# Graph attention with exponentials left unscaled and inverse sums applied to the node products

## The chip, the cores and the metric

The kernel runs on 1 core of one Trainium2 chip, as one launch. The metric is the device time of the launch in microseconds (us); lower is better. The engines: PE (TensorE, with PEld its weight loads), DVE (VectorE), ACT (ScalarE), POOL (GpSimd), SP (SyncE, which here issues most DMAs). Each runs its own instructions in program order and waits for the others by semaphores.

## The reference, cut to what matters

Two graph transformer blocks over 625 nodes of width 768 and 20000 edges. The change lies in the graph attention of the second block, in the first of its two layers (8 heads of 128 columns):

```python
def gat_layer(x, W, att_src, att_dst, bias, src, dst, heads, out_ch, concat):
    n = x.shape[0]
    h = (x @ W.T).reshape(n, heads, out_ch)
    a_src = jnp.einsum('nhc,hc->nh', h, att_src)
    a_dst = jnp.einsum('nhc,hc->nh', h, att_dst)
    e = jax.nn.leaky_relu(a_src[src] + a_dst[dst], 0.2)
    m = jax.ops.segment_max(e, dst, num_segments=n)
    ex = jnp.exp(e - m[dst])
    denom = jax.ops.segment_sum(ex, dst, num_segments=n)
    alpha = ex / (denom[dst] + 1e-16)
    out = jax.ops.segment_sum(alpha[:, :, None] * h[src], dst, num_segments=n)
    ...
h = gat_layer(x, W1, ..., heads=8, out_ch=128, concat=True)
h = jax.nn.relu(h)
out = gat_layer(h, W2, ..., heads=1, out_ch=768, concat=True)
```

Before it the block has another attention (called mix here), and behind it a routed feed-forward layer of 8 experts, which takes about the second half of the time.

## The kernel before

**How the numbers are held.** Every 32-bit product on PE is made of three matmuls: each operand is a pair of a rounded upper half (made by ACT, `upper`, L358) and the rest (made by DVE, `lower`, L361: source minus upper half). `mm3` (L340) multiplies hi x hi, hi x lo, lo x hi. PE writes its results into 8 PSUM banks, handed out in turn by `ring.next`, which makes PE wait until the bank's last content was evicted.

**The graph attention as a dense one.** Nodes are padded to 640, 5 tiles (`TT`) of 128. Edge counts were made into a dense matrix of logs, `edge_log` (a tile of destinations by 640 sources). The first layer goes over 4 groups (`grp`) of 2 heads. In a group, a *unit* is one head and one tile of destinations: 10 units a group, 40 (`N1`) in all. Units of the same head are closed in *pairs* of `n` tiles (tiles 0 and 1, 2 and 3, and tile 4 alone), 6 a group, 24 in all.

**Steps of a unit**, with their lag in ticks behind the tick at which the unit enters (a tick is one turn of the loops over `i`, L2072, L2200 and L2372, which each engine has for itself):

- 0, ACT: raw edge scores by a Relu (`raw_edges`, L2170); POOL has added the source row to the edge logs (`terms`, L1999), a step that waits for the peak of two units before.
- 1, DVE: `peak` (L2329): joins the two, and finds minus the maximum.
- 2, ACT: `exponent` (L2176), with the row's sum into `total`.
- 3, DVE: sum + 1e-16, its reciprocal, times `has_edge` (L2396 to L2398).
- 4, ACT: the exponentials times that inverse, per destination, which lies on the partitions (L2232).
- 5, PE: five transposes (`turn_unit`, L2046), so that sources lie on the partitions.
- 6, ACT and DVE: upper and lower half of the transposed exponentials into `exT`, a spare part of the tiles `weight_hi` and `weight_lo` (so a row `weight_hi<-bank 128x384` is such a step, and `weight_hi<-weight_raw` is a weight's).
- 7, PE, at the last unit of a pair: the z product (L2093), nodes `hg` times `exT`, 15 matmuls; the result has the head's columns on the partitions and destinations along the free side.
- 8, ACT: Relu with bias (L2214) and upper half of z; DVE: lower half (`zT_lo`).

**Work put between, by tables of ticks:** the output projection of z by the second layer's weights (`Y_AT`, PE 12 matmuls a tile, DVE adds it), the node projections of the next group (`PREPARE`, PE 18 matmuls a step, ACT its upper half at L2158, DVE its lower half at L2301 and four dots for the scores), the turning and spreading of the source rows (`TURNED`, L2015; `SPREAD`, L354, L2145), and the splitting of weights into halves (`SPLIT`, L304, L314). Within a tick PE's order is: output projection, z product, source rows, transposes, node projections. ACT's is: z, upper halves of the exponentials, scaling, exponent, source rows, raw edges, projections, weights. DVE's is: lower half of z, lower halves of the exponentials, inverse sum, peak, output projection, node projection, weights. After the last tick the second layer begins with the scores of the last output projection.

## Time and profile before

| what | us |
|---|---|
| median of 3 runs | 1976.0 |
| lowest, highest run | 1969.53, 1976.93 |
| span of the profiled execution, first to last instruction | 1967.6 |
| PE busy in it | 1855.2 (94%) |
| DVE busy | 1295.7 (66%) |
| ACT busy | 934.8 (48%) |
| POOL busy | 151.5 (8%) |
| mean granted clock of PE | 0.973 of full speed |

How to read it: the shares are means over the whole program. The stage of the change takes about a tenth of it, and there the three engines are near each other; the stretches of that stage tell more than the table. Granted clock is the share of its full speed that the chip let PE run at; its two levels are 1.2 and 2.4 GHz. Ends of matmuls are modelled: durations of neighbours overlap, so the distance between two starts is the better price.

### The profile page before, as it was taken

The page shows a single profiled execution, that of the slowest core. Times are in us where ns is not written, and L with a number is a line of the kernel's source. Part 1 is how long each engine was busy: PE and PEld are TensorE (multiplying, and loading weights), DVE is VectorE, ACT ScalarE, POOL GpSimd, SP SyncE. Part 2 cuts the span into 40 slices and gives each one's busy share as a digit, 9 for nine tenths or more (in the row PEclk, how much of TensorE's full clock was granted, in tenths as well). Part 3 has the DMA queues.
Part 4 walks back from the last instruction along what each step waited for, and adds up shares of the span by engine and source line. Part 5 has one row for each costly group of instructions (what it writes and reads, how often), then busy time and mean ns, then how long its engine had stood idle before and what let it go on. Part 6 is the DMA issues. An engine that isn't in the chain of part 4 may idle for free.

```text
span 1967.6 us, 30950 instructions
## 1 busy us (share of the span) xinstructions
PE 1855.2 (94%) x12197; PEld 1758.9 (89%) x12198; DVE 1295.7 (66%) x2485; ACT 934.8 (48%) x1551; POOL 151.5 (8%) x127
## 2 busy tenths in 40 slices
PE   6987999999999999788799999999999999999998
PEld 5876789998889999787699999999999999999998
DVE  7997767555345656888865744456566667676886
ACT  2331222325134536878534232345555556666776
POOL 0000000004000023323100000000101001001010
PEclk9997999999999999899799999999999999999999
DMA  3110002101112112010131132154656566676795
GB/s 117 49 49 1 25 25 105 33 25 60 62 49 89 73 39 94 23 38 17 65 123 61 63 104 73 73 207 183 220 193 221 214 217 240 219 261 245 283 328 199
DMA packets 36844, 234.30 MB, mean 119 GB/s; under 512 B 5964, under 2 KB 7366, under 8 KB 14680
## 3 DMA queue, kind: packets, MB, share of 16 engines
q1 hardware_dynamic: 31366, 217.41, 30.8%
q0 software_dynamic: 2656, 8.99, 2.0%
q10 hardware_dynamic: 2674, 5.87, 0.8%
q8 instruction: 99, 1.62, 0.3%
q14 instruction: 49, 0.40, 0.1%
HBM read 221.91 MB, written 10.35 MB: 118 GB/s over the span
## 4 chain that ended last, share of the span: by engine, by line
PE 43%; issue 3%; DVE 3%; DMA 1%; ACT 1%; POOL 0%; ACTq 0%; POOLq 0%; DVEq 0%
PE bank L2734 8%; PE bank L341 7%; PE bank L342 7%; PE bank L343 7%; PE bank L2735 4%; PE bank L2746 3%; PE bank L2750 2%; PE bank L2738 2%; PE bank L2747 2%; PE bank L2749 1%; PE bank L2737 1%; DVE weight_lo L314 1%; PE bank L2692 0%; DMA out<-ffn_y,slot_token 0%; DMA weight_raw_fifth<-in_ffn_w 0%
## 5 line engine op out<-in xcount | busy, mean ns | idle before, releaser
L314 DVE TENSOR_TENSOR weight_lo<-weight_raw,weight_hi 128x2304 fp32r<-128x2304 f32 (+1 forms) x155 | 392.3, 2534 | 53.5 <-ACT weight_hi L304 53.2
L304 ACT ACTIVATE weight_hi<-weight_raw 128x2304 fp32r<-128x2304 f32 (+1 forms) x155 | 323.3, 2087 | 69.1 <-DMA weight_raw<-in_ffn_w 48.3
L341 PE MATMUL bank<-xT_hi,weight_hi 128*128 128x320 f32 (+1 forms) x576 | 182.8, 317 | 1.6 <-DVE xT_lo L362 1.4
L342 PE MATMUL bank<-xT_lo,weight_hi 128*128 128x320 f32 (+1 forms) x576 | 178.0, 309 | 0.0
L343 PE MATMUL bank<-xT_hi,weight_lo 128*128 128x320 f32 (+1 forms) x576 | 177.7, 309 | 0.0
L341 PE MATMUL bank<-weight_hi,xT_hi 128*128 128x384 f32 (+1 forms) x480 | 161.4, 336 | 11.2 <-DVE weight_lo L314 6.2
L3114 DVE TENSOR_TENSOR hidden_tmp<-hidden_tmp,bank 128x160 f32<-128x160 f32 (+5 forms) x192 | 65.6, 342 | 159.5 <-ACT hidden_tmp L2897 159.5
L342 PE MATMUL bank<-weight_lo,xT_hi 128*128 128x384 f32 (+1 forms) x480 | 157.3, 328 | 0.0
L343 PE MATMUL bank<-weight_hi,xT_lo 128*128 128x384 f32 (+1 forms) x480 | 157.0, 327 | 0.0
L615 PE MATMUL bank<-one_hot_dst,one_hot_src 125*128 125x313 f16 x800 | 123.5, 306 | 15.2 <-ACT packed_counts L629 7.9
L2897 ACT ACTIVATE hidden_tmp<-bank,ffn_b_by_load 128x160 f32<-128x160 f32 (+5 forms) x192 | 73.6, 404 | 119.8 <-PE bank L2738 114.2
L341 PE MATMUL bank<-weight_hi,hidden_hi 128*128 128x384 f32 (+1 forms) x366 | 124.7, 341 | 0.0
L342 PE MATMUL bank<-weight_lo,hidden_hi 128*128 128x384 f32 (+1 forms) x366 | 123.8, 338 | 0.0
L615 PEld LDWEIGHTS bank<-one_hot_dst,one_hot_src 125*128 125x128 f16 x800 | 75.0, 100 | 52.3 <-DVE one_hot_dst L587 17.3
L2734 PE MATMUL bank<-xT_hi,weight_hi 128*128 128x512 f32 (+3 forms) x390 | 117.3, 361 | 3.4 <-DVE hidden_tmp L3114 1.7
L343 PE MATMUL bank<-weight_hi,hidden_lo 128*128 128x384 f32 (+1 forms) x348 | 117.7, 338 | 0.0
L341 PEld LDWEIGHTS bank<-xT_hi,weight_hi 128*128 128x128 f32 x576 | 110.1, 191 | 7.1 <-issue 4.2
L2734 PE MATMUL bank<-xT_lo,weight_hi 128*128 128x320 f32 (+3 forms) x390 | 110.5, 350 | 5.9 <-DVE xT_hi L3069 4.9
L342 PEld LDWEIGHTS bank<-xT_lo,weight_hi 128*128 128x128 f32 x576 | 110.3, 191 | 0.0
L343 PEld LDWEIGHTS bank<-xT_hi,weight_lo 128*128 128x128 f32 x576 | 110.1, 191 | 0.0
L341 PEld LDWEIGHTS bank<-weight_hi,xT_hi 128*128 128x128 f32 x480 | 93.3, 194 | 13.4 <-DVE weight_lo L314 7.0
L2735 PE MATMUL bank<-xT_hi,weight_lo 128*128 128x256 f32 (+3 forms) x390 | 97.7, 250 | 0.0
(496 smaller groups left out, 5062.4 us busy)
## 6 DMA issues: line engine op xcount, KB each, us to landing
weight_raw<-in_ffn_w SPq DMA_DIRECT2D x111, 1152.0 KB, 5.1
weight_raw_fifth<-in_ffn_w SPq DMA_DIRECT2D x25, 1152.0 KB, 5.1
weight_raw<-in_shared_w SPq DMA_DIRECT2D x16, 1152.0 KB, 5.0
weight_raw<-in_mix_kv SPq DMA_DIRECT2D x8, 1152.0 KB, 5.0
weight_raw<-in_gat_w SPq DMA_DIRECT2D x8, 768.0 KB, 4.2
weight_raw<-in_mix_q SPq DMA_DIRECT2D x4, 1152.0 KB, 5.0
weight_raw<-in_mix_out SPq DMA_DIRECT2D x4, 1152.0 KB
weight_raw<-in_gnn_w SPq DMA_DIRECT2D x4, 1152.0 KB, 5.1
```

Of the source, the lines that this page charges most:

```text
L304: act.activation(upper_, whole_, ACT.Copy).then_inc(*w_hi.one())
L314: dve.tensor_tensor(lower_, whole_, upper_.bitcast(F32), ALU.subtract).then_inc(*w_lo.one())
L341: pe.matmul(dst, a[0], b[0], start=first, stop=False)
L342: pe.matmul(dst, a[0], b[1], start=False, stop=False)
L343: return pe.matmul(dst, a[1], b[0], start=False, stop=last)
L615: end = pe.matmul(edge_banks[t][:, 0:TM], hot_src[:, j % HOT, tok(t)], hot_dst[:, j % HOT, 0:TM], start=(i == 0), stop=(i == CHUNK_E - 1))
L2734: pe.matmul(both, hi[:, k, :], x_e[:, k, :, 0:width], start=(k == 0), stop=False)
L2735: pe.matmul(first, lo[:, k, :], x_e[:, k, 0, 0:width], start=False, stop=False)
L2738: end = pe.matmul(both, hi[:, k, :], x_e[:, k, :, 0:width], start=False, stop=True)
L2746: pe.matmul(both, hi[:, k, :], h[:, k, :, 0:width], start=(first and k == 0), stop=False)
L2897: act.activation(ht[:, i % 3, 0:CAPS[e]], r_banks[i][:, 0:CAPS[e]], ACT.Identity, bias=b1r[:, e, i % (3 * NCH):i % (3 * NCH) + 1]).then_in ...
L3114: dve.tensor_tensor(part, part, r_banks[i][:, width:2 * width], ALU.add).then_inc(*r_sum.one())
```

## The change

What it does:

- The exponentials are not scaled. The copy at lag 4 on ACT goes, and the transposes move from lag 5 to 3, the halves from 6 to 4, the z product from 7 to 5.
- Instead z is multiplied by the inverse sums. There the destinations lie along the free side, so the inverses are needed as rows, the same on all partitions: at lag 3, once a pair, DVE adds `least_sum` and takes the reciprocals of the pair's `n` sums; at lag 4 PE transposes each column, broadcast to 128 columns; at lag 5 ACT copies the bank into one tile, `inverse` (named `edge_terms` in rows, since it is a spare part of that tile); at lag 6 DVE multiplies z's bank with it into `zt`, ACT makes the Relu in place and the upper half, DVE the lower half.
- `least_sum`, made once, is 1e-16 where a destination has edges and 5e37 where it has none; it takes the place of `has_edge` in this layer. `has_edge` stays for the second layer.
- Node projections: ticks 5, 6, 7, 7, 8 of the first group and 4, 5, 5, 6, 7 of the two others, before 6, 6, 7, 7, 8 of each. Output projections stand 2 or 3 ticks earlier for the last three tiles of group 2 and all of group 3 (groups are counted from 0), and three weights are split 2 or 4 ticks later. The last lag is 8 instead of 10. The raw edges have 5 slots instead of 7, z's halves 3 instead of 2.
- On ACT, z's steps move behind the upper halves of the exponentials; on DVE the product stands first and z's lower half behind peak and sums.

```diff
@@ layout
+        least_sum = sb("gat_least_sum", [P, TT], F32, gat)
-        ZS, XS = 7, DEPTH
+        ZS, XS = 5, DEPTH
-        zT = pair("gat_zT", [P, 2, 2, 2 * P], gat)
+        zT = pair("gat_zT", [P, 3, 2, 2 * P], gat)
+        inverse = count_f32[:, 2 * TP:2 * TP + 2 * P]
@@ tables
-        LAST_LAG = 10
+        LAST_LAG = 8
-        PREPARE = {6: (0, 1), 7: (2, 3), 8: (4,)}
-        Y_AT = {10 * grp + tick: (grp, t) for grp in range(4) for t, tick in enumerate((12, 13, 18, 19, 21) if grp < 3 else (12, 13, 16, 17, 18))}
+        PREPARE = {5: (0,), 6: (1,), 7: (2, 3), 8: (4,)}, {4: (0,), 5: (1, 2), 6: (3,), 7: (4,)}
+        Y_AT = {10 * grp + tick: (grp, t) for grp in range(4) for t, tick in enumerate({2: (12, 13, 16, 17, 18), 3: (10, 11, 14, 15, 16)}.get(grp, (12, 13, 18, 19, 21)))}
-        SPLIT = {10: c0 + 2, 12: c0 + 3, 14: c0 + 4, 20: c0 + 5, 24: c0 + 6, 28: c0 + 7}
+        SPLIT = {10: c0 + 2, 12: c0 + 3, 18: c0 + 4, 20: c0 + 5, 28: c0 + 6, 30: c0 + 7}
@@ def tensor():
-                q = pair_closing(i, 7)
+                q = pair_closing(i, 5)
...
-                    bank = ring.next(z_relu.at(q + 1))
+                    bank = ring.next(z_scaled.at(q + 1))
...
-                u = unit(i, 5)
+                u = unit(i, 3)
                 if u is not None:
-                    turn_unit(u, e_scaled.at(u + 1))
+                    turn_unit(u, e_exp.at(u + 1))
+                q = pair_closing(i, 4)
+                if q is not None:
+                    grp, h, t0, n = pairs_of[q]
+                    pe.wait_ge(*e_summed.at(q + 1))
+                    bank = ring.next(inverse_kept.at(q + 1))
+                    inverse_banks.append(bank)
+                    for t in range(n):
+                        end = pe.transpose(bank[:, t * P:(t + 1) * P], total[:, grp % 2, h, t0 + t:t0 + t + 1].broadcast_to([P, P]), ident[:, :])
+                    end.then_inc(*inverse_full.one())
@@ def scalar():
-                q = pair_closing(i, 8)
-                if q is not None:
...
-                    act.activation(zt[:, q % 2, 0:n * P], z_banks[q][:, 0:n * P], ACT.Relu, bias=b1[:, 2 * grp + h:2 * grp + h + 1]).then_inc(*z_relu.one())
...
-                u = unit(i, 6)
+                u = unit(i, 4)
...
-                u = unit(i, 4)
-                if u is not None:
-                    grp, h, t = units[u][0:3]
-                    e = edge_w[:, u % ZS, :]
-                    act.wait_ge(*e_summed.at(u + 1))
-                    act.activation(e, e, ACT.Copy, scale=total[:, grp % 2, h, t:t + 1]).then_inc(*e_scaled.one())
+                q = pair_closing(i, 5)
+                if q is not None:
+                    n = pairs_of[q][3]
+                    act.wait_ge(*inverse_full.at(q + 1))
+                    if q:
+                        act.wait_ge(*z_scaled.at(q))
+                    act.activation(inverse[:, 0:n * P], inverse_banks[q][:, 0:n * P], ACT.Copy).then_inc(*inverse_kept.one())
+                q = pair_closing(i, 6)
+                if q is not None:
+                    grp, h, t0, n = pairs_of[q]
+                    act.wait_ge(*z_scaled.at(q + 1))
+                    z = zt[:, q % 2, 0:n * P]
+                    act.activation(z, z, ACT.Relu, bias=b1[:, 2 * grp + h:2 * grp + h + 1]).then_inc(*z_relu.one())
+                    act.wait_ge(*z_relu.now())
+                    if grp:
+                        act.wait_ge(*sums_before(q))
+                    upper(at(zT, ALL, z_slot(q), h, slice(0, n * P)), z).then_inc(*z_hi.one())
@@ def vector():
-                q = pair_closing(i, 8)
+                q = pair_closing(i, 6)
+                if q is not None:
+                    grp, h, t0, n = pairs_of[q]
+                    dve.wait_ge(*z_full.at(q + 1))
+                    dve.wait_ge(*inverse_kept.at(q + 1))
+                    if q >= 2:
+                        dve.wait_ge(*z_lo.at(q - 1))
+                    dve.tensor_tensor(zt[:, q % 2, 0:n * P], z_banks[q][:, 0:n * P], inverse[:, 0:n * P], ALU.mult).then_inc(*z_scaled.one())
+                u = unit(i, 4)
+                if u is not None:
+                    turned_lower(u, at(exT, ALL, u % XS, ALL, ALL))
+                u = unit(i, 1)
+                if u is not None:
+                    peak(u, *units[u][0:3])
+                if pair_closing(i, 3) is not None:
+                    grp, h, t0, n = pairs_of[pair_closing(i, 3)]
+                    sums = total[:, grp % 2, h, t0:t0 + n]
+                    dve.wait_ge(*e_exp.at(i - 3 + 1))
+                    own_step(dve.tensor_tensor(sums, sums, least_sum[:, t0:t0 + n], ALU.add))
+                    dve.reciprocal(sums, sums).then_inc(*e_summed.one())
                 if q is not None:
                     grp, h, t0, n = pairs_of[q]
                     dve.wait_ge(*z_hi.at(q + 1))
                     lower(at(zT, ALL, z_slot(q), h, slice(0, n * P)), zt[:, q % 2, 0:n * P]).then_inc(*z_lo.one())
-                u = unit(i, 3)
-                if u is not None:
-                    grp, h, t = units[u][0:3]
-                    tot = total[:, grp % 2, h, t:t + 1]
-                    dve.wait_ge(*e_exp.at(u + 1))
-                    own_step(dve.tensor_scalar(tot, tot, 1e-16, None, ALU.add))
-                    own_step(dve.reciprocal(tot, tot))
-                    dve.tensor_tensor(tot, tot, has_edge[:, t:t + 1], ALU.mult).then_inc(*e_summed.one())
```

How instructions stand in a row shows it better at two places. On ACT, tick 16 and the start of 17, before: z's Relu and upper half, two rounded pieces of turned exponentials, scaling (L2232), exponent, raw edges, and the projections of the next group but one:

```order
L2214 ACTIVATE gat_z<-bank,gat_b 128x128
L359 ACTIVATE gat_zT_hi<-gat_z 128x128
L359 ACTIVATE weight_hi<-bank 128x384
L359 ACTIVATE weight_hi<-bank 128x256
L2232 ACTIVATE gat_edge<-gat_edge,gat_total 128x640
L2176 ACTIVATE gat_edge,gat_total<-gat_edge,gat_minus_peak 128x640
L2170 ACTIVATE gat_edge<-gat_src_row,gat_dst_bias 128x640
L2158 ACTIVATE gat_h_hi<-bank 128x256 x2
L2214 ACTIVATE gat_z<-bank,gat_b 128x128
L359 ACTIVATE gat_zT_hi<-gat_z 128x128
```

On ACT in the change, tick 14 behind its halves and the start of 15 (L2234 copies the inverses, L2240 is z's Relu, L2188 the exponent):

```order
L2234 ACTIVATE edge_terms<-bank 128x128
L2240 ACTIVATE gat_z<-gat_z,gat_b 128x128
L359 ACTIVATE gat_zT_hi<-gat_z 128x128
L2188 ACTIVATE gat_edge,gat_total<-gat_edge,gat_minus_peak 128x640
L2180 ACTIVATE gat_edge<-gat_src_row,gat_dst_bias 128x640
L2168 ACTIVATE gat_h_hi<-bank 128x256
L359 ACTIVATE weight_hi<-bank 128x384
L359 ACTIVATE weight_hi<-bank 128x256
L2240 ACTIVATE gat_z<-gat_z,gat_b 128x128
L359 ACTIVATE gat_zT_hi<-gat_z 128x128
```

The copy of 640 columns is gone, a copy of 128 columns of inverses stands ahead of z, and one projection follows the raw edges where two did.

On DVE, tick 15 and the start of 16, before, with z's lower half ahead of the exponentials' lower halves, and three small steps ahead of each peak (ISA, L2329):

```order
L362 TENSOR_TENSOR gat_zT_lo<-gat_z,gat_zT_hi 128x256
L362 TENSOR_TENSOR weight_lo<-bank,weight_hi 128x384
L362 TENSOR_TENSOR weight_lo<-bank,weight_hi 128x256
L2396 TENSOR_SCALAR gat_total<-gat_total 128x1
L2397 RECIPROCAL gat_total<-gat_total 128x1
L2398 TENSOR_TENSOR gat_total<-gat_total,gat_has_edge 128x1
L2329 ISA gat_edge,gat_minus_peak<-gat_edge,edge_terms 128x640
L2329 ISA gat_minus_peak 128x1
L362 TENSOR_TENSOR gat_zT_lo<-gat_z,gat_zT_hi 128x128
```

And tick 14 in the change (L2404 is the product with the inverses, L2343 the peak, L2415 and L2416 the sums):

```order
L2404 TENSOR_TENSOR gat_z<-bank,edge_terms 128x128
L362 TENSOR_TENSOR weight_lo<-bank,weight_hi 128x384
L362 TENSOR_TENSOR weight_lo<-bank,weight_hi 128x256
L2343 ISA gat_edge,gat_minus_peak<-gat_edge,edge_terms 128x640
L2343 ISA gat_minus_peak 128x1
L2415 TENSOR_TENSOR gat_total<-gat_total,gat_least_sum 128x2
L2416 RECIPROCAL gat_total<-gat_total 128x2
L362 TENSOR_TENSOR gat_zT_lo<-gat_z,gat_zT_hi 128x128
L2313 TENSOR_TENSOR gat_h_lo<-bank,gat_h_hi 128x256
```

z's lower half moved from ahead of the peak to behind it and the sums, right ahead of the node projection's steps.

## Rows read from the trace of the kernel before

**Rows 1.** The page: the span of the profiled execution

```profile
span 1967.6 us, 30950 instructions
```

**Rows 2.** Stages: microseconds busy per engine (instructions), granted clock, DMA share, GB/s

```profile
773.19:797.08 23.89, 19.52 (x152) 18.60 (x150) 19.78 (x87) 19.27 (x42) 6.26 (x4) 0.93 0.65 227
797.08:848.91 51.83, 42.69 (x293) 40.59 (x292) 40.45 (x133) 40.43 (x86) 15.66 (x10) 0.90 0.00 1
848.91:901.13 52.22, 45.48 (x303) 42.70 (x304) 43.08 (x138) 42.44 (x89) 15.58 (x10) 0.91 0.12 42
901.13:965.60 64.47, 56.70 (x369) 53.40 (x368) 55.06 (x158) 48.67 (x106) 15.65 (x10) 0.94 0.09 27
```

**Rows 3.** Waits of PE, 773 to 966 us: waiter, releaser: total us, times, longest

```profile
PE bank L341 <- DVE weight_lo L362: 13.3, 10, 3.2
PE bank L2015 <- DVE gat_scores L2278: 2.9, 1, 2.9
...
PE bank L2046 <- ACT gat_edge L2232: 2.5, 2, 1.5
```

**Rows 4.** PE in order of time: start us, us, line, operation, shape [idle before]

```profile
860.46 0.71 PE L2046 MATMUL bank<-identity,gat_edge 128*128 128x128 f32 x5
860.92 0.42 PE L341 MATMUL bank<-weight_hi,gat_zT_hi 128*128 128x384 f32 x1
...
863.13 0.71 PE L2046 MATMUL bank<-identity,gat_edge 128*128 128x128 f32 x5
...
867.22 0.33 PE L341 MATMUL bank<-weight_hi,gat_h_hi 128*128 128x128 f32 x1 [0.37 <-DVE weight_lo L362]
...
868.95 0.74 PE L2046 MATMUL bank<-identity,gat_edge 128*128 128x128 f32 x5
872.91 0.33 PE L341 MATMUL bank<-weight_hi,gat_h_hi 128*128 128x128 f32 x1 [3.23 <-DVE weight_lo L362]
```

**Rows 5.** ACT in order of time, one tick and its z steps

```profile
869.47 0.75 ACT L359 ACTIVATE weight_hi<-bank 128x384 fp32r<-128x384 f32 x2
870.10 0.83 ACT L2232 ACTIVATE gat_edge<-gat_edge,gat_total 128x640 f32<-128x640 f32 x1
870.82 0.82 ACT L2176 ACTIVATE gat_edge<-gat_edge,gat_minus_peak 128x640 f32<-128x640 f32 x1
...
872.35 0.36 ACT L2214 ACTIVATE gat_z<-bank,gat_b 128x128 f32<-128x128 f32 x1
...
872.96 0.75 ACT L359 ACTIVATE weight_hi<-bank 128x384 fp32r<-128x384 f32 x2
```

**Rows 6.** DVE in order of time, columns as in rows 4

```profile
912.72 1.15 DVE L362 TENSOR_TENSOR gat_zT_lo<-gat_z,gat_zT_hi 128x256 fp32r<-128x256 f32 x1
...
917.57 0.14 DVE L2396 TENSOR_SCALAR gat_total<-gat_total 128x1 f32<-128x1 f32 x1
...
918.06 0.83 DVE L2329 CUSTOM_DVE_ANT_0 gat_edge<-gat_edge,edge_terms 128x640 f32<-128x640 f32 x1
...
918.82 0.42 DVE L362 TENSOR_TENSOR gat_zT_lo<-gat_z,gat_zT_hi 128x256 fp32r<-128x256 f32 x1
919.15 0.88 DVE L362 TENSOR_TENSOR weight_lo<-bank,weight_hi 128x384 fp32r<-128x384 f32 x2
```

**Rows 7.** POOL in order of time, beside them

```profile
912.02 1.57 POOL L1999 TENSOR_TENSOR edge_terms<-gat_edge_log,gat_src_row 128x640 f32<-128x640 f32 x1 [1.40 <-DVE gat_minus_peak L2329]
...
919.04 1.61 POOL L1999 TENSOR_TENSOR edge_terms<-gat_edge_log,gat_src_row 128x640 f32<-128x640 f32 x1 [1.41 <-DVE gat_minus_peak L2329]
```

**Rows 8.** The two stretches behind the 3.2 us waits, columns as in rows 2

```profile
821.90:826.00 4.10, 4.10 (x24) 4.10 (x25) 3.48 (x12) 4.07 (x9) 1.82 (x2) 0.64 0.00 0
872.90:877.00 4.10, 4.08 (x25) 4.09 (x26) 3.53 (x13) 3.05 (x7) 1.84 (x2) 0.66 0.00 0
```

**Rows 9.** Groups by shape: busy us, mean ns | idle before

```profile
L2301 DVE TENSOR_TENSOR gat_h_lo<-bank,gat_h_hi 128x256 fp32r<-128x256 f32 x15 | 6.3, 423 | 9.9 <-ACT gat_h_hi L2158 9.8
L2158 ACT ACTIVATE gat_h_hi<-bank 128x256 fp32r<-128x256 f32 x15 | 5.7, 383 | 19.7 <-PE bank L343 19.7
```

More of the change, by code:

```diff
@@ L1838, in graph_attention @@
          att_in, h_full, h_hi, h_lo, scored, score_turned, score_hi, score_lo, rows_full, rows_kept,
-         e_acted, e_made, e_exp, e_summed, e_scaled, ex_turned, ex_hi, ex_lo, z_full, z_relu, z_hi, z_lo,
+         e_acted, e_made, e_exp, e_summed, z_scaled, inverse_full, inverse_kept, ex_turned, ex_hi, ex_lo, z_full, z_relu, z_hi, z_lo,
          y_full, y_added, scored2, h2_hi, h2_lo, o_full, o_added) = sigs(*names)
@@ L1892, in graph_attention @@
         h_banks, turn_banks, row_banks, ex_banks, z_banks, y_banks, o_banks = [], [], [], [], [], [], []
+        inverse_banks = []
         units, pairs_of = [], []
@@ L1933, in preparations @@
             if i < N1 and i // 10 < 3:
-                for step in PREPARE.get(i % 10, ()):
+                for step in PREPARE[i >= 10].get(i % 10, ()):
                     yield i // 10 + 1, step
@@ L1944, in z_slot, with sums_before @@
         def z_slot(q):
+            return pairs_of[q][2] // 2
+        def sums_before(q):
             grp, h, t0, n = pairs_of[q]
-            return (3 * grp + t0 // 2) % 2
-        def sums_after(q):
-            grp, h, t0, n = pairs_of[q]
-            return y_full.at(2 * (grp * TT + t0 + n))
+            return y_full.at(2 * ((grp - 1) * TT + t0 + n))
         def w1_chunk(grp):
@@ L2175, in exponent @@
                 act.wait_ge(*e_made.at(u + 1))
+                if grp > 1 and t == 0:
+                    act.wait_ge(*aggregated(grp - 2))
                 act.activation(e, e, ACT.Exp, bias=minus_peak[:, grp % 2, h, t:t + 1], scale=-1.0,
@@ L2207, in scalar @@
                     act.dma_start(slots_dram[:, 0:D].rearrange("(t p) d -> p t d", p=P), x[:, :, :]).then_inc(*x_kept.dma())
-                q = pair_closing(i, 8)
-                if q is not None:
-                    grp, h, t0, n = pairs_of[q]
-                    act.wait_ge(*z_full.at(q + 1))
-                    if q >= 2:
-                        act.wait_ge(*z_lo.at(q - 1))
-                    act.activation(zt[:, q % 2, 0:n * P], z_banks[q][:, 0:n * P], ACT.Relu, bias=b1[:, 2 * grp + h:2 * grp + h + 1]).then_inc(*z_relu.one())
-                    act.wait_ge(*z_relu.now())
-                    if q >= 4:
-                        act.wait_ge(*sums_after(q - 4))
-                    upper(at(zT, ALL, z_slot(q), h, slice(0, n * P)), zt[:, q % 2, 0:n * P]).then_inc(*z_hi.one())
                 if i in Y_AT and Y_AT[i][1] == TT - 1:
@@ L2320, in edge_logs @@
                 dve.wait_ge(*dve_own.now())
+                own_step(dve.tensor_scalar(least_sum[:, :], edge_peak[:, :], -1.0, 5.0e37, ALU.is_lt, ALU.mult))
+                own_step(dve.tensor_scalar(least_sum[:, :], least_sum[:, :], 1e-16, None, ALU.add))
                 dve.tensor_scalar(has_edge[:, :], edge_peak[:, :], -1.0, None, ALU.is_ge).then_inc(*edges_known.one())
@@ L2387, in vector @@
                     lower(at(zT, ALL, z_slot(q), h, slice(0, n * P)), zt[:, q % 2, 0:n * P]).then_inc(*z_lo.one())
-                u = unit(i, 6)
-                if u is not None:
-                    turned_lower(u, at(exT, ALL, u % XS, ALL, ALL))
-                u = unit(i, 3)
-                if u is not None:
-                    grp, h, t = units[u][0:3]
-                    tot = total[:, grp % 2, h, t:t + 1]
-                    dve.wait_ge(*e_exp.at(u + 1))
-                    own_step(dve.tensor_scalar(tot, tot, 1e-16, None, ALU.add))
-                    own_step(dve.reciprocal(tot, tot))
-                    dve.tensor_tensor(tot, tot, has_edge[:, t:t + 1], ALU.mult).then_inc(*e_summed.one())
-                u = unit(i, 1)
-                if u is not None:
-                    peak(u, *units[u][0:3])
                 if i == FIRST_PART + 1:
```

4 lines of the change are left out of this document (2 added, 2 removed).

## The prediction

> **What bounds the kernel now.** Read first how long the stage takes and who is busy in it. One execution spans 1967.6 us [rows 1], and the loop that is changed lies between 773 and 966 us. In the three stretches from one spreading of source rows to the next, and on to the last output projection (51.83, 52.22 and 64.47 us), PE is busy 42.69, 45.48 and 56.70 us: it leads, but sits idle 9.1, 6.7 and 7.8 us, 23.7 us together. DVE follows with 40.45, 43.08 and 55.06, ACT with 40.43, 42.44 and 48.67 [rows 2]. So no engine is the bound throughout; it changes from tick to tick.
>
> Then read what PE waits for. The largest entry is the lower half of the turned exponentials, 13.3 us in 10 waits, the longest 3.2; the scores of the last node projection cost 2.9 once, and the scaled exponentials 2.5 in two [rows 3]. One of the 3.2 us waits is seen in order of time: PE ends its five transposes after 868.95 and begins the next z product only at 872.91 [rows 4]. DVE, named as releaser, is not the slow one: it subtracts what ACT has rounded, and ACT in these ticks runs without a gap. One tick of ACT goes from 869.47 to 872.35, 2.88 us: 0.63 for rounding the turned exponentials, 0.72 for the copy that scales them, and 1.53 for the exponent and the raw edges; the z steps of one tile add 0.61 [rows 5]. That is 3.5 us, while PE needs 1.73 for such a z product and about 0.46 for five transposes [rows 4]. In these ticks ACT is the bound; in the projection ticks PE is, since before two projections stood in one tick there.
>
> A gap costs a second time. Behind both 3.2 us waits the granted clock is 0.64 and 0.66 over 4.10 us [rows 8], the lower level (1.2 GHz) for most of it. Over the three stretches it is 0.90, 0.91 and 0.94 [rows 2].
>
> **The change, part by part.** The sum is made on the profiled execution; the median of the runs, 1976.0, lies 8.4 us above its span. A difference of less than 0.5%, 9.9 us, can't be told from none here. I put the difference on the median.
>
> 1. *The scaling copy goes.* 40 copies at 0.72 leave ACT, 28.8 us [rows 5]. In come 24 copies of spread inverses, nearest to the 256-column copy from a bank, 383 ns [rows 9], at most 9.2 us. An ACT tick falls from 2.88 to 2.16, with z steps and an inverse to about 3.2 at most. Then PE (z product, transposes, an output projection of 2.21 in some [rows 4]) or DVE is the longer. Both 3.2 us waits go: -6.4. Of the other 6.9 us of that entry (bounds 0 and 6.9) I take two thirds, since most are ACT ticks too and some are DVE's own: -4.6.
> 2. *Transposes take the exponentials unscaled*, two ticks earlier. The 2.5 us of waits on scaled exponentials can't stand as they do; the exponent is ready a tick before. -2.5, bounds 0 and -2.5.
> 3. *Clock.* With the two gaps go their slow stretches: 4.10 x 0.36 + 4.10 x 0.34 = -2.9 [rows 8]. Bounds: 0 if some other gap takes their place, and -13.8 if the clock never fell (0.10 x 51.83 + 0.09 x 52.22 + 0.06 x 64.47 [rows 2]).
> 4. *PE gains work.* 40 transposes of a broadcast column. Five transposes take 0.46 from 860.46 to 860.92 [rows 4], 0.09 each: +3.7. No cover: PE leads. The order has them behind the exponentials' transposes of the tick, so what is queued behind them are node projections and the next output projection.
> 5. *DVE.* Three small steps a unit go, 0.49 from 917.57 to 918.06 [rows 6], 40 times: -19.6. In come 24 products of a bank with the inverses, nearest to the 256-column subtraction from a bank, 423 ns [rows 9], and 24 pairs of small steps, two thirds of 0.49: 24 x (0.42 + 0.33) = +18.0. Even, before the next point. The two steps that make the least sums come ahead of the loop, while DVE waits for PE: nothing.
> 6. *DVE against POOL.* The subtraction that makes the lower half of z reads two tiles in SBUF. It took 0.42 where it began 0.22 ahead of POOL's sum, and 1.15 where it began 0.70 behind [rows 6, 7]: it waited till POOL was through. POOL starts just after each peak (its sum waits for it). Before, z's subtraction stood first in a tick, away from that. Now it stands behind peak and small sums. Right behind the peak it still comes first; where the sums lie between (two of six in a group, eight in all) it starts some 0.33 later, 0.1 behind POOL, and waits about 1.57 - 0.1 - 0.3 = 1.1 [rows 6, 7]. 8 x 1.1 = 8.8 on DVE; a quarter reaches PE, which leads: +2.2, bounds 0 and 24 x 1.1 = 26.4.
> The Trainium skill ("SBUF — State Buffer", section Who interferes with whom) says that a DVE instruction with two SBUF inputs and a GpSimd instruction that reads SBUF block each other wholly, and that the order of issue decides who. By that rule, the trace agrees, the product with the inverses, one input from a bank, is free of it, and the lower half of z is not.
> 7. *Node projections spread over ticks* (one, two, one, one instead of two, two, one), output projections moved to the ticks that lost a projection. Nothing is added; PE's own work stays, and it fills ticks in which PE waited. That gain is in term 1. The scores behind a projection take DVE the same time, and the 2.9 us wait before the first turned scores [rows 3] stays: there the last projection stands right ahead of it in both orders. Attention rows and weights land ahead of the earlier projections by several us: nothing.
> 8. *Lag 8 instead of 10.* No work less; two units' transposes and a z product come out of the tail into the first group, where PE works without them too. Nothing by itself.
>
> Sum: -6.4 - 4.6 - 2.5 - 2.9 + 3.7 + 2.2 = **-10.5 us**, 1976.0 - 10.5 = 1965.5.
>
> **Rivals.**
> *DVE becomes the bound.* If all six z subtractions of a group meet POOL (z's upper half is late, ACT now makes it behind a DVE step), DVE's busy time in the second stretch is 43.08 - 4.9 + 4.5 + 6 x 1.1 = 49.3, in the first 46.7 [rows 2, 6, 9]. With the 3 us that it can't fill anyway, since it waits for PE and ACT, that is 52.3 and 49.7 against 52.22 and 51.83: some 2 us gained, and 1 in the tail, which DVE nearly fills now (55.06 of 64.47). 1973. For it: DVE is busy only 2.2 and 2.4 us less than PE now. Against: a z's upper half has the time of rounding and peak, some 1.5 us, to get ready.
> *The waits go further and the clock stays up.* The idle 23.7 us fall by two thirds (15.8), 1.5 more ahead, and half of the 13.8 us of clock (6.9), less 3.7: -20.5, 1955.5. For it: loads of a tick are now near each other. Against: the gap at the first group's start, where the output weights are rounded at the same tick as before, stays and pulls the clock down there.
> *The longer z chain, slower.* z passed from PE to ACT; now PE's spread inverses are copied by ACT (0.38), DVE multiplies (0.42), and only then ACT has its z steps (0.61). There is one inverse tile and ACT takes its steps in order: while it waits for the product, exponent and raw edges are queued behind it, and PE waits for the exponent one tick on. Each of 24 pairs whose wait is exposed costs 0.38 + 0.42 + 0.61 = 1.41 [rows 5, 9]. It decides from 8 exposed pairs on (8 x 1.41 = 11.3 against 10.5). With 16: 22.6 - 10.5 = +12, 1988. Against it: DVE has the product first in its tick, and ACT rounds exponentials for 0.63 ahead of the wait.
>
> **How the numbers follow.** Forecast 0.5, with its own range 1959 to 1972; DVE bound 0.2 (1973); clock up 0.2 (1955.5); longer chain 0.1 (1988). The forecast lies just past the 0.5% line (1966.1), so its half is split, 0.28 faster and 0.22 same. Faster 0.28 + 0.2 = 0.48, same 0.22 + 0.2 = 0.42, slower 0.10. The range 1954 to 1977 leaves out the slower rival and a little below.
>
> **What would show it.** Right: no wait of 3 us in the middle of a group, a granted clock above 0.93 in the two middle stretches, each 3 us or more shorter than 51.83 and 52.22; ACT's busy share there down by 5 us a stretch; two of six z subtractions near 1.5 us and the others at 0.42. DVE bound: most of the six above 1 us and PE waiting for DVE's lower half as before. Longer chain: ACT idle ahead of z's Relu, released by DVE's product. Wrong altogether: stretches as long as before with ACT idle, or a new wait of PE for inverse sums.

## The result, and the profile after

| | before | after |
|---|---|---|
| median of 15 runs, us | 1970.56 | 1977.9 |
| lowest, highest | 1968.73, 1977.19 | 1972.53, 1982.03 |
| span of the profiled execution | 1967.6 | 1980.2 |
| ratio after to before, 95% interval | | 1.0033 [1.0024, 1.0043] |

The change makes the kernel 0.33% slower by the ratio, which is 6.5 us (the two medians lie 7.3 us apart), where 10.5 us less was forecast. The 1977.9 us lie outside the range of 1954 to 1977, though only by 0.9 us. That it is so near is luck: the forecast started from 1976.0, the median of 3 runs of the kernel before, and over 15 runs that median is 1970.56. As a change, the forecast missed by 17 us.

The page of the kernel after, its span (for rows 1) and the busy time of each engine:

```profile
span 1980.2 us, 31018 instructions
...
PE 1858.9 (94%) x12237; PEld 1763.4 (89%) x12238; DVE 1293.0 (65%) x2439; ACT 914.4 (46%) x1535; POOL 151.5 (8%) x127
```

ACT has lost 20 us of work, DVE 3, and only PE has gained, 4 us, which the forecast had counted. The rest of the loss must lie in waits. The same four stretches of the loop after, columns as in rows 2:

```profile
772.17:805.50 33.33, 26.63 (x181) 25.26 (x179) 23.06 (x88) 19.22 (x47) 7.83 (x5) 0.85 0.46 163
805.50:858.47 52.97, 43.79 (x302) 41.76 (x302) 41.92 (x123) 35.97 (x82) 15.68 (x10) 0.90 0.01 1
858.47:910.47 52.00, 44.83 (x314) 42.35 (x314) 41.58 (x125) 35.07 (x82) 15.69 (x10) 0.93 0.10 37
910.47:973.74 63.27, 53.60 (x357) 51.13 (x357) 52.34 (x141) 41.81 (x100) 15.66 (x10) 0.95 0.10 32
```

The first stretch is 9.4 us longer than in rows 2, the second 1.1 longer, the third 0.2 shorter, the tail 1.2 shorter. ACT is busy 4.5 and 7.4 us less in the two middle stretches, and they are no shorter: what ACT gave up was not handed on. Who is waited for now (waits of PE, 773 to 975 us; columns as in rows 3):

```profile
PE bank L341 <- DVE gat_z L2404: 6.9, 2, 4.2
PE bank L2047 <- DVE gat_z L2404: 6.9, 3, 4.7
PE bank L341 <- DVE weight_lo L362: 6.8, 4, 2.1
...
PE bank L2047 <- DVE x L1818: 2.3, 1, 2.3
PE bank L2016 <- DVE gat_scores L2290: 2.1, 1, 2.1
```

The waits of PE before, two lines that rows 3 don't show (the first is for a bank of z, which ACT emptied then):

```profile
PE bank L2046 <- ACT gat_z L2214: 2.3, 1, 2.3
PE bank L2046 <- DVE weight_lo L362: 2.1, 2, 1.6
```

and those of ACT after:

```profile
ACT gat_z L2240 <- DVE gat_z L2404: 26.4, 15, 4.3
```

The lower halves, 13.3 us in 10 waits before [rows 3], are down to 6.8 in 4 (and 2.1 us of the transposes' waits for them to 0.9). In their place stands L2404, the product of z with the spread inverses, the new instruction on DVE: PE waits 13.8 us for it in 5 waits, up to 4.7, and ACT 26.4 us in 15. PE doesn't read that product's output in these waits. It wants the *bank* that the product reads, for other work: `ring.next` gives a bank out again only when it was emptied. Before, ACT emptied the bank of z, and PE waited 3.1 us in all for that (the 2.3 above, and 0.8 in two waits of L341); now DVE does.

Why DVE is late is seen in its order of time around one such wait (start us, us, line, op, shape [idle before]):

```profile
859.84 0.14 DVE L2415 TENSOR_TENSOR gat_total<-gat_total,gat_least_sum 128x2 f32<-128x2 f32 x1
860.01 0.17 DVE L2416 RECIPROCAL gat_total<-gat_total 128x2 f32<-128x2 f32 x1
863.04 2.43 DVE L314 TENSOR_TENSOR weight_lo<-weight_raw,weight_hi 128x1536 fp32r<-128x1536 f32 x1 [2.86 <-ACT weight_hi L304]
865.39 0.41 DVE L2404 TENSOR_TENSOR gat_z<-bank,edge_terms 128x256 f32<-128x256 f32 x1
```

The spread inverses for this product were copied by ACT, and the z product itself was there:

```profile
857.19 0.28 PE L343 MATMUL bank<-weight_hi,gat_h_lo 128*128 128x256 f32 x1
...
858.29 0.36 ACT L2234 ACTIVATE edge_terms<-bank 128x256 f32<-128x256 f32 x1
...
859.36 1.36 ACT L2155 ACTIVATE gat_src_row<-bank 128x320 f32<-128x320 f32 x4
860.80 0.83 ACT L2180 ACTIVATE gat_edge<-gat_src_row,gat_dst_bias 128x640 f32<-128x640 f32 x1
861.54 1.47 ACT L304 ACTIVATE weight_hi<-weight_raw 128x1536 fp32r<-128x1536 f32 x1
```

Its inputs are ready at 858.65, and it begins at 865.39, 6.7 us later. The product is first in its tick of DVE. But the tick before it ends with a weight's lower half (`SPLIT`, here at i = 20), for which DVE waits till ACT has rounded that weight, and in this tick ACT does so last, behind the four copies of the spread source rows. That costs DVE 2.86 us idle and 2.43 of work, all ahead of the product. The same happens at i = 10 (the weight's lower half begins at 809.84, behind 3.21 us idle) and at i = 30 (915.03, behind 2.85). All five waits of PE for the product stand behind such a lower half: 4.7, 2.7 and 4.2 us behind these three, and 1.1 us each behind those at i = 18 and 28, for which DVE didn't wait but worked 2.21 us (852.04 and 904.03). PE, behind the one at i = 20:

```profile
862.69 0.47 PE L343 MATMUL bank<-weight_hi,gat_zT_lo 128*128 128x384 f32 x1
865.86 0.44 PE L341 MATMUL bank<-weight_hi,gat_zT_hi 128*128 128x384 f32 x1 [2.71 <-DVE gat_z L2404]
```

It waits 2.71 us for a bank in the midst of an output projection whose data it has.

Such gaps cost again, through the clock. Around this one, and behind the 4.7 us wait that ends at 812.64 (windows, columns as in rows 2):

```profile
859.50:863.20 3.70, 3.66 (x14) 2.86 (x12) 0.81 (x5) 3.62 (x7) 2.40 (x2) 0.54 0.00 0
866.00:870.00 4.00, 4.00 (x17) 3.90 (x18) 3.96 (x9) 3.81 (x9) 1.54 (x1) 0.57 0.33 88
812.60:816.60 4.00, 3.96 (x14) 3.96 (x15) 3.96 (x9) 3.95 (x9) 1.56 (x1) 0.50 0.00 0
```

In the 4 us behind the gap of 2.71 PE is busy throughout, at a granted clock of 0.57, mostly the 1.2 GHz level: 4.0 x 0.43 = 1.7 us more. But the clock was low ahead of this gap too, 0.54 in the 3.7 us before it, where PE had waited only 1.1 us (at 854.64) and 1.0 us (at 858.47) shortly before. So the 1.7 us can't be put down to the one gap. Behind the 4.7 us wait it is plainer: the clock was 1.00 from 806 to 808, where PE stopped, and 0.50 in the 4 us behind, 2.0 us more.

### The profile page after: what moved, and what is told of

The parts are those of the page before. It is cut to its first block, busy times and chain, and to the rows that moved or that the text cites. A ratio compares the mean times of both kernels' runs of the same rounds, so it can differ in the third digit from the quotient of the medians.

```text
span 1980.2 us, 31018 instructions
## 1 busy us (share of the span) xinstructions
PE 1858.9 (94%) x12237; PEld 1763.4 (89%) x12238; DVE 1293.0 (65%) x2439; ACT 914.4 (46%) x1535; POOL 151.5 (8%) x127
## 4 chain that ended last, share of the span: by engine, by line
PE 43%; issue 3%; DVE 3%; DMA 1%; ACT 1%; POOL 0%; ACTq 0%; POOLq 0%; DVEq 0%
PE bank L2753 8%; PE bank L341 7%; PE bank L343 7%; PE bank L342 7%; PE bank L2754 4%; PE bank L2765 3%; PE bank L2769 2%; PE bank L2757 2%; PE bank L2766 2%; PE bank L2768 1%; PE bank L2756 1%; DMA out<-ffn_y,slot_token 1%; DVE weight_lo L314 1%; PE bank L2711 0%; DMA weight_raw_fifth<-in_ffn_w 0%
## 5 line engine op out<-in xcount | busy, mean ns | idle before, releaser
L314 DVE TENSOR_TENSOR weight_lo<-weight_raw,weight_hi 128x2304 fp32r<-128x2304 f32 (+1 forms) x155 | 392.2, 2534 | 54.8 <-ACT weight_hi L304 54.6
L341 PE MATMUL bank<-xT_hi,weight_hi 128*128 128x320 f32 (+1 forms) x576 | 182.9, 318 | 1.6 <-DVE xT_lo L362 1.4
L341 PE MATMUL bank<-weight_hi,xT_hi 128*128 128x384 f32 (+1 forms) x480 | 162.2, 338 | 16.9 <-DVE weight_lo L314 6.2
L342 PE MATMUL bank<-weight_lo,xT_hi 128*128 128x384 f32 (+1 forms) x480 | 158.4, 330 | 0.0
L343 PE MATMUL bank<-weight_hi,xT_lo 128*128 128x384 f32 (+1 forms) x480 | 158.4, 330 | 0.0
L341 PE MATMUL bank<-weight_hi,hidden_hi 128*128 128x384 f32 (+1 forms) x366 | 125.0, 342 | 0.4 <-DVE weight_lo L314 0.4
L341 PEld LDWEIGHTS bank<-xT_hi,weight_hi 128*128 128x128 f32 x576 | 110.2, 191 | 7.0 <-issue 4.2
L341 PEld LDWEIGHTS bank<-weight_hi,xT_hi 128*128 128x128 f32 x480 | 94.1, 196 | 19.9 <-DVE weight_lo L314 7.0
```

Of the source, the lines that this page charges most:

```text
L314: dve.tensor_tensor(lower_, whole_, upper_.bitcast(F32), ALU.subtract).then_inc(*w_lo.one())
L341: pe.matmul(dst, a[0], b[0], start=first, stop=False)
L342: pe.matmul(dst, a[0], b[1], start=False, stop=False)
L343: return pe.matmul(dst, a[1], b[0], start=False, stop=last)
```

## The experiments

The times are medians over 5 rounds, with the ratio to the kernel before, run in the same rounds, and its 95% interval. The ratio is not the quotient of the medians. The kernels ran in several sets of rounds, so they are compared by their ratios here: 0.1% is 2.0 us. "Loop" goes from the end of PE's last product for the other attention to the end of the last output projection, the four stretches together but for 0.2 us, from one profiled execution each: 192.2 us before, 201.6 after. Two profiles of a loop that should be alike differ by 1 or 2 us, so a loop alone settles no difference of that size.

| kernel | median, us | ratio | loop, us |
|---|---|---|---|
| after | 1977.9 | 1.0033 [1.0024, 1.0043] | 201.6 |
| a_noinv: no inverse chain | | | 178.1 |
| a_nomult: chain without product | | | 183.3 |
| a_split | 1969.78 | 0.9994 [0.9978, 1.0010] | 192.5 |
| b_split | 1972.69 | 1.0010 [0.9998, 1.0023] | 191.7 |
| a_zfirst | 1968.82 | 0.9992 [0.9978, 1.0007] | 192.8 |
| a_prep | 1988.2 | 1.0092 [1.0071, 1.0114] | 208.5 |
| b_head | 1970.96 | 0.9997 [0.9983, 1.0011] | 193.1 |
| a_sums | 1977.71 | 1.0042 [1.0030, 1.0055] | 200.1 |
| a_split_one | 1966.38 | 0.9973 [0.9958, 0.9988] | 189.1 |
| a_split_added | 1966.72 | 0.9980 [0.9966, 0.9993] | 190.0 |
| a_best | 1964.82 | 0.9974 [0.9964, 0.9985] | 185.4 |
| a_late | 1960.58 | 0.9955 [0.9942, 0.9968] | 184.0 |

**1. What the gains are, and what the chain costs.** The kernel after without any of the inverse chain (sums, transposes of inverses, copy, product); ACT takes z from its bank again. The output is not divided by the sums.

```diff
-                    bank = ring.next(z_scaled.at(q + 1))
+                    bank = ring.next(z_relu.at(q + 1))
...
-                        end = pe.transpose(bank[:, t * P:(t + 1) * P], total[...].broadcast_to([P, P]), ident[:, :])
...
-                    act.activation(inverse[:, 0:n * P], inverse_banks[q][:, 0:n * P], ACT.Copy)
...
-                    act.activation(z, z, ACT.Relu, ...)
+                    act.activation(z, z_banks[q][:, 0:n * P], ACT.Relu, ...)
...
-                    dve.tensor_tensor(zt[...], z_banks[q][:, 0:n * P], inverse[:, 0:n * P], ALU.mult)
...
-                    own_step(dve.tensor_tensor(sums, sums, least_sum[:, t0:t0 + n], ALU.add))
-                    dve.reciprocal(sums, sums)
```

> The changed kernel with the inverse sums left out of the first graph layer (no sums, transposes, copies or products; ACT takes its Relu from z's bank, so its output isn't divided): all else in place. If the longer z chain is what the change costs: the 3.7 us of transposes, the waits for the product and part of the clock go, 12 to 16 us less than the changed kernel, 1962 to 1966. If the shorter lag and the placement are what costs: 5 us less, 1973.

With values that are not divided a later layer takes another path, so the whole time (3575 us) says nothing; the loop can be read. Then the same with the product alone left out, while sums, transposes and copies stay:

> The changed kernel with DVE's product alone left out: sums, transposes and copies of the inverses stay, but ACT takes z's Relu from its bank, so the output isn't divided, and the routed layer behind runs into its overflow loop, so the whole time says nothing; read is the loop, from the last projection of the other attention to the last output projection. It was 192.2 us before, 201.6 in the changed kernel, 178.1 without the whole chain. If the product's place between PE and ACT is the cost: about 185. If DVE's and PE's added work is: about 196.

The loop as one window: before, after, a_noinv and a_nomult, in this order (columns as in rows 2):

```profile
773.35:965.59 192.24, 164.23 (x1112) 155.12 (x1110) 158.35 (x513) 150.81 (x320) 53.16 (x34) 0.92 0.14 49
```

```profile
772.17:973.74 201.57, 168.85 (x1152) 160.49 (x1150) 158.91 (x474) 132.06 (x308) 54.87 (x35) 0.92 0.14 47
```

```profile
775.99:954.06 178.07, 157.91 (x1112) 152.41 (x1110) 139.62 (x404) 125.60 (x284) 55.10 (x35) 0.92 0.15 53
```

```profile
772.05:955.37 183.32, 161.55 (x1152) 155.08 (x1150) 151.93 (x452) 131.25 (x308) 54.91 (x35) 0.93 0.15 51
```

So the unscaled exponentials, with the new tables, give 14.2 us (192.24 - 178.07). The chain without its product costs 5.2, of which 3.6 are PE's 40 transposes (161.55 - 157.91). The product costs 18.3 (201.6 - 183.3), though it is busy for only 24 steps of about 0.4, and DVE is idle 42.7 us of this loop. Net +9.3 in these profiles, +6.5 in the runs.

Emptying z's bank isn't free on ACT either. In a_nomult, where ACT does it, PE waits 7.0 us for that in 3 waits, up to 2.9:

```profile
PE bank L341 <- ACT gat_z L2242: 4.1, 2, 2.3
PE bank L2047 <- ACT gat_z L2242: 2.9, 1, 2.9
```

Against 13.8 with the product, PE's waits for this bank explain 6.8 of the 18.3 us directly.

**2. The weights' splits a tick earlier.** If it is the product's place behind a split, then moving the splits out of the ticks with source rows must bring most of it back, in the kernel after alone. a_split:

```diff
-        SPLIT = {10: c0 + 2, 12: c0 + 3, 18: c0 + 4, 20: c0 + 5, 28: c0 + 6, 30: c0 + 7}
+        SPLIT = {9: c0 + 2, 12: c0 + 3, 18: c0 + 4, 19: c0 + 5, 28: c0 + 6, 29: c0 + 7}
```

> The changed kernel with the weight splits of ticks 10, 20 and 30 one tick earlier (9, 19, 29), where DVE has them ahead of the spreading of source rows. Theory N (z's bank is freed only by DVE's product, which in those ticks stands behind a weight's lower half of 1.7 to 2.4 us): of PE's 11.6 us of waits for the product behind the three spreadings at least 2 us each go, and part of the slow clock behind them: 5 to 8 us less than the changed kernel, about 1971. Theory P (the cost sits in the projections' placement): 1977, no change.

It brought 7.7 us: 0.9994 against 1.0033, the kernel before's time. The same in the kernel before (10 to 9, 20 to 19), b_split:

> The kernel before with two weight splits one tick earlier (9 and 19 instead of 10 and 20), as in the variant of the change. Theory N: there z's bank is freed by ACT ahead of the split, so little is gained: within 2 us of before. Rival (the split in the ticks of the spreading costs any kernel as much): 4 to 6 us less than before, and the gain of the variant says nothing on the z product.

There it brings nothing, 1.0010 with 1 inside the interval. So the place of the splits costs where DVE has z's bank to empty, and not where ACT has.

**3. The product ahead of the split, on DVE alone.** The splits stay in their ticks for ACT. DVE alone takes each one tick later, right behind the product:

```diff
                     dve.tensor_tensor(zt[:, q % 2, 0:n * P], z_banks[q][:, 0:n * P], inverse[:, 0:n * P], ALU.mult)
+                if i - 1 in SPLIT:
+                    weight_lo(SPLIT[i - 1])
...
-                if i in SPLIT:
-                    weight_lo(SPLIT[i])
```

> The changed kernel with nothing but DVE's order changed: a weight's lower half comes one tick later, right behind the z product instead of ahead of it; ACT's order and all ticks stay. Theory N as refined by the trace (z is full, but DVE stands waiting for the weight's upper half, 2.9 to 3.2 us, and then takes 2.4 for the lower one, before it frees z's bank): most of PE's 13.8 us of waits for the product go, 6 to 9 us less than the changed kernel, 1969 to 1971, like the variant with earlier splits. Rival (what helped there was the split leaving the ticks in which ACT keeps the spread rows): less than 3 us, 1976.

No instruction is added, dropped or made shorter, and ACT's and PE's orders are those of after. It brought 8.1 us (0.9992), as much as a_split. DVE in order of time, at the same place of the program:

```profile
856.78 0.17 DVE L2418 RECIPROCAL gat_total<-gat_total 128x2 f32<-128x2 f32 x1
856.89 0.42 DVE L2404 TENSOR_TENSOR gat_z<-bank,edge_terms 128x256 f32<-128x256 f32 x1
859.62 2.47 DVE L314 TENSOR_TENSOR weight_lo<-weight_raw,weight_hi 128x1536 fp32r<-128x1536 f32 x1 [2.31 <-ACT weight_hi L304]
```

DVE still waits for ACT's rounding, 2.31 us, but with z's bank emptied: the wait costs little where nothing hangs on what is queued behind it. PE's waits for the product are down from 13.8 us to 0.2, and the loop from 201.6 to 192.8.

That is 8.8 of the product's 18.3 us. The other 9.5, up to a_nomult's 183.3, stay, and their cause was not taken apart. The waits say where they fall: PE waits 4.4 us once for a weight's lower half (L314), where it waited 0.8 in a_nomult, and its products (L341) wait 10.8 us in 6 for the exponentials' lower halves, against 4.2 in 4. ACT, which rounds both ahead of DVE, still waits 17.4 us in 13 for the product.

**4. The placement of the node projections.** The forecast took it as worth nothing of its own. a_prep gives the kernel after the old table:

```diff
-        PREPARE = {5: (0,), 6: (1,), 7: (2, 3), 8: (4,)}, {4: (0,), 5: (1, 2), 6: (3,), 7: (4,)}
+        PREPARE = {6: (0, 1), 7: (2, 3), 8: (4,)}, {6: (0, 1), 7: (2, 3), 8: (4,)}
```

> The changed kernel with the node projections back in the ticks of before (two, two, one in ticks 6 to 8 of every group). Theory P (a projection behind two others finds its bank held by the turned exponentials, whose lower halves DVE makes after eight dots; 2.1, 1.9 and 1.7 us of PE waits and the slow clock behind them): 5 to 8 us less than the changed kernel, about 1971. Theory N: no change, or slower, since the loads bunch again: 1978 to 1982.

It is 11.6 us slower than after by the ratios (10.3 by the medians). The waits for z's bank grow (waits of PE, a_prep):

```profile
PE bank L341 <- DVE gat_z L2404: 14.4, 5, 4.2
...
PE bank L2047 <- DVE gat_z L2404: 7.7, 3, 4.7
```

22.1 us against 13.8. The loop is 6.9 us longer than after's, and not evenly: 3.8 us in the first stretch (773.93 to 811.05, 37.1 against 33.3), 3.1 in the third (864.01 to 919.11, 55.1 against 52.0), none in the others. The other way round, b_head gives the kernel before the new first row of the table (5: 0; 6: 1; 7: 2, 3; 8: 4) for its first group only:

> The kernel before with one edit of the change: in the first group the projections stand in ticks 5, 6, 7, 7, 8 instead of 6, 6, 7, 7, 8. Theory P: the first group alone loses 2 to 4 us, 1973 to 1975. Theory N: no difference from before, within 1 us of 1970.6.

Nothing, 0.9997; its first stretch (772.18 to 795.25) is 23.1 us, against 23.7 of the same piece before. And a_split_one adds to a_split a table with never two projections in a tick, in the later groups:

```diff
-        PREPARE = ..., {4: (0,), 5: (1, 2), 6: (3,), 7: (4,)}
+        PREPARE = ..., {4: (0,), 5: (1,), 6: (2,), 7: (3,), 8: (4,)}
```

> The variant with earlier splits (1969.8), and the projections of the two later groups at exactly one a tick (4 to 8, with none doubled). If PE's two waits of 1.9 and 1.7 us behind the doubled projections (DVE makes eight dots before it frees the exponentials' bank) are a cost: 3 to 5 us less, 1965. If they only stand in for waits elsewhere: within 1.5 us, 1969.

0.9973 against a_split's 0.9994. The two intervals overlap, but the loop is shorter too, by 3.4 us.

**5. The collision of z's lower half with POOL.** a_sums puts DVE's small sums ahead of the peak, so that the lower half of z comes right behind it and starts before POOL:

```diff
-                u = unit(i, 1)
-                if u is not None:
-                    peak(u, *units[u][0:3])
                 if pair_closing(i, 3) is not None:
                     ...
                     dve.reciprocal(sums, sums).then_inc(*e_summed.one())
+                u = unit(i, 1)
+                if u is not None:
+                    peak(u, *units[u][0:3])
```

> The changed kernel with DVE's two small steps on the sums ahead of the peak instead of behind it, so that z's lower half follows the peak at once. The six lower halves of 1.65 to 1.80 us fall to 0.42 and 0.29, 8 us of DVE time. If DVE was not the bound there (a quarter reaches PE, as forecast): about 2 us less, 1976. If DVE was: 6 to 8 us less, 1971. Sums stuck behind POOL instead would show as small steps of over 1 us.

The group of z's lower halves (shortest / median / longest ns, and shapes), first after, then a_sums:

```profile
L362 DVE TENSOR_TENSOR gat_zT_lo<-gat_z,gat_zT_hi x24: 285/422/1805, 789.3 to 971.0; 128x256 fp32r<-128x256 f32 x16, 128x128 fp32r<-128x128 f32 x8
```

```profile
L362 DVE TENSOR_TENSOR gat_zT_lo<-gat_z,gat_zT_hi x24: 285/420/426, 787.2 to 968.8; 128x256 fp32r<-128x256 f32 x16, 128x128 fp32r<-128x128 f32 x8
```

All collisions are gone, DVE is busy 6.3 us less in the loop, and the time is the same (1.0042 against 1.0033, intervals overlapping). The collisions are real and cost nothing here.

**6. The wait at the head.** After the change PE waits 2.3 us once for L1818, the addition of the first attention's last output into `x`. a_split_added does this addition a tick earlier (i = 4 instead of 5), on top of a_split:

> The variant with earlier splits (1969.8), and DVE's additions of the last two tiles of the other attention one tick earlier (4 instead of 5), which free the banks that PE waits 2.3 us for at the loop's head, with a slow clock behind it. If the shorter lag costs at the head by this: 3 to 4 us less, 1966. If the head is bound by DVE's dots anyway: within 1.5 us, 1969.

0.9980 against 0.9994 for a_split; the intervals overlap, the loop is 2.5 us shorter, and the wait is gone from the profile. It looks like the size of that wait, but the difference is within the measurement's error, so the gain is not shown.

**7. Together, and one step further.** a_best is a_split with the one-a-tick table, the earlier addition and the sums first:

> The change with all single edits together: splits earlier, projections at one a tick, the other attention's additions one tick earlier, sums ahead of the peak. Effects were -7.7, -4, -3 and 0 us, partly on the same waits. If they add up: 1962. If DVE is what bounds the middle groups by then, the sums' edit (8 us less DVE time in its waits for POOL) shows now too: 1960. If they share one wait: 1965.

a_late moves, on top of this, ACT's two z steps behind its exponent and raw edges of the tick, and takes z's lower half on DVE a tick later, first in the tick:

```diff
-                q = pair_closing(i, 6)
-                    act.wait_ge(*z_scaled.at(q + 1))
-                    ... Relu and upper half of z ...
                 u = unit(i, 2)
                 ...
                     raw_edges(u, *units[u][0:3])
+                q = pair_closing(i, 6)
+                    act.wait_ge(*z_scaled.at(q + 1))
+                    ... Relu and upper half of z ...
```

> The same, and z's steps on ACT behind the raw edges of their tick, z's lower half on DVE one tick later and first in it. ACT waited 26.4 us for the product in the changed kernel, with exponent and raw edges queued behind. If that wait costs PE anything: 3 to 5 us less than with the edits alone, 1957 to 1960. If PE's waits were for banks only: no change, or a little slower at the tail, where the output projection comes right behind z's lower half.

Waits of ACT for the product, a_best and then a_late (26.4 us in 15 after):

```profile
ACT gat_z L2240 <- DVE gat_z L2404: 19.4, 11, 4.6
```

```profile
ACT gat_z L2250 <- DVE gat_z L2409: 4.5, 1, 4.5
```

a_late takes 1960.58 us, 0.9955 of the kernel before: the fastest of all, 8.9 us under before and 15.4 under after by the ratios. It is 4.2 us under a_best in the same rounds, but the two intervals overlap slightly, and of this the loop shows only 1.4 us (185.4 to 184.0), though ACT's waits for the product are down by 14.9. So whether these waits of ACT cost PE anything is not shown.

## Why the prediction was wrong, point by point

**The step that failed** is term 5, "Even, before the next point", with the sentence that dismissed the third rival: "DVE has the product first in its tick". DVE's work did come out even (158.4 us busy in the loop before, 158.9 after); what failed is that the product was priced by its duration alone. What it took over was the emptying of z's bank, from ACT to DVE, and its place there is behind whatever ends the tick before: the weight's lower half, with its wait for ACT. No term asks when the z bank comes free. The product costs +18.3 us in the loop (a_nomult to after), where this term and the next gave +2.2. Of these, 8.8 are shown to be that place behind a weight's lower half: a_zfirst and a_split take it away from two sides (each back to 0.999), and b_split shows that it is not the splits themselves. The other 9.5 stay open.

**Of the signs named in advance**, those of a wrong forecast came: the two middle stretches are as long as before (52.97 and 52.00 against 51.83 and 52.22) with ACT idle, and ACT stands ahead of z's Relu for DVE's product. ACT's busy time there fell by 4.5 and 7.4 us, as forecast.

**The third rival** had the right side, chance 0.1, and a part of the mechanism. ACT does wait for the product, 26.4 us in 15 waits; what that costs PE is not shown (a_late). Its price, 1.41 a pair as the chain's own length, found no match: the chain costs 23.5 us (5.2 + 18.3) in 24 pairs, 0.98 each on average, and PE's 13.8 us of waits for the product are five, of 1.1 to 4.7 us. And the one way of the loss that is shown, PE waiting for a bank, the rival did not have.

**Terms 1 and 2** were right in kind, and term 1 too large. Both 3.2 us waits for the lower halves are gone (-6.4), and so are the waits on scaled exponentials. But of the other 6.9 us in that entry, of which 4.6 were to go, 6.8 are still there in the kernel after, and 4.4 in a_noinv. A new wait at the head (L1818, 2.3 us) ate what term 2 gave. Terms 1 to 3 were 16.4 us together; the loop without the chain is 14.2 shorter, so their sum was near.

**Term 3**, the clock: -2.9 were forecast, and its bound of 0 came in, "if some other gap takes their place". The granted clock is 0.85, 0.90, 0.93 and 0.95 after, against 0.93, 0.90, 0.91 and 0.94 in rows 2.

**Term 4** was right: 40 transposes, 3.6 us busy on PE, 3.7 forecast.

**Term 6** was near on the collisions after and wrong on the rest. Two of six z subtractions of a group were to wait, eight in all, 1.1 us each; six of 24 took 1.65 to 1.80 us, some 1.4 too long each, all others 0.42 or less. But the kernel before was not free of them: five of its 24 took 1.05 to 1.69 us (two are at 912.72, in rows 6, and at 905.16), so the change added less DVE time than the term says. In rows of after, POOL, and DVE beside it:

```profile
814.26 1.56 POOL L2000 TENSOR_TENSOR edge_terms<-gat_edge_log,gat_src_row 128x640 f32<-128x640 f32 x1 [3.63 <-DVE gat_minus_peak L2343]
```

```profile
814.04 0.15 DVE L2415 TENSOR_TENSOR gat_total<-gat_total,gat_least_sum 128x1 f32<-128x1 f32 x1
...
814.31 1.80 DVE L362 TENSOR_TENSOR gat_zT_lo<-gat_z,gat_zT_hi 128x256 fp32r<-128x256 f32 x1
```

The quarter that was to reach PE (+2.2) was nought: a_sums. This also does away with the first rival (DVE as the bound): DVE is idle 42.7 us in the loop. It is late in an order, not short of time.

**Term 7**, "Nothing is added", took the placement as worth nothing of its own. In the new order the old table costs 11.6 us (a_prep), more than any other edit. For the first group alone, the one whose row was tried in both orders, it is 3.8 us in the new order and nothing in the old one (b_head). Two projections in a tick lengthen the time between two ticks in which DVE can empty banks. That reading fits the longer waits for z's bank in a_prep, but was not taken apart further.

**Term 8** was right: the first stretch is longer and the tail shorter, as two units' work moved from the one to the other. Of the 9.4 us by which the first stretch grew, 2.9 remain without the chain (26.8 in a_noinv against 23.9); the tail of a_noinv is 5.1 shorter.

**What stays open.** What makes up the 9.5 us of the product's cost that a_zfirst does not bring back. Why PE waits 2.1 to 2.3 us for some lower halves still, in a_late too, and how the 5.2 us of the chain without its product part into PE's transposes (3.6) and the rest (1.6, within what two profiles differ by).

## What to carry to other kernels

When a step moves to another engine, price not its duration but the thing that it frees: ask which bank or buffer comes free by it, and what stands ahead of it in that engine's order, waits of the last tick included. A step that waits for another engine belongs behind everything that others wait for, which costs no instruction; here such a reordering of one engine was worth 0.4%. And when a change of tables and a change of work come together, run the tables against both kinds of work: the same row of a table was worth 3.8 us with one and nothing with the other, in one profile each.

## What the runs showed of the hardware

- A DVE step with two inputs in SBUF that would start 0.05 us behind POOL's sum (814.31 against 814.26) took 1.80 us instead of 0.42, whereas one right behind the peak, without the 0.27 us of small sums between, kept its 0.42. So some 0.3 us of order decides about 1.3 us of work. The product, with one input from a bank, took 0.42 even where it lay wholly within a sum of POOL (939.72, within 938.74 to 940.32). The Trainium skill ("SBUF — State Buffer", section Who interferes with whom) says that a DVE instruction with two SBUF inputs contends with a GpSimd instruction that reads SBUF, and one with at most one SBUF input does not, and that the order of issue decides who is blocked; the runs agree.
- Behind a gap of 4.7 us on PE the granted clock was 0.50 over 4.0 us of work, behind one of 4.2 us it was 0.62 over 4.2 us (917.80 to 922.00), behind gaps of 3.2 us 0.64 and 0.66 over 4.1 us [rows 8]; it was 1.00 ahead of each. That is 1.4 to 2.0 us more, about four tenths of the gap again. And it fell without a long gap: it was 0.54 over the 3.7 us from 859.50, behind two gaps of 1.1 and 1.0 us in the 6 us before, in which it was 1.00.
